# Half of the output projection moved into the second half of attention, keys into its first half, and the next group's weight splits into attention

## The chip, the cores and the metric

The kernel runs on one core of a Trainium2 chip. The metric is the device time of one launch in microseconds (us). Its engines are named as in the profile: PE is TensorE (PEld its weight loads), DVE is VectorE, ACT is ScalarE, POOL is GpSimd and SP is SyncE, which here only issues DMAs.

## The reference

One block of a transformer with adaptive LayerNorm, in fp32, for 4 batches of 512 rows of 1024 features. What matters here is the attention part:

```python
h = _layernorm(x, axis=-1) * (1 + ca) + sa
x = x + ga * _L0_attn_ref(h, L0_attn_wq, L0_attn_wk, L0_attn_wv, L0_attn_wo)
...
q = (x @ wq).reshape(B, S, N_Q_HEADS, HEAD_DIM)
k = (x @ wk).reshape(B, S, N_KV_HEADS, HEAD_DIM)
v = (x @ wv).reshape(B, S, N_KV_HEADS, HEAD_DIM)
q = _rope(q, pos)
k = _rope(k, pos)
...
scores = jnp.where(allowed[None, None, None], scores, neg)
attn = jax.nn.softmax(scores, axis=-1)
out = jnp.einsum('bhgqs,bshd->bqhgd', attn, v).reshape(B, S, N_Q_HEADS * HEAD_DIM)
return out @ wo
```

There are 32 query heads of 128 features, 8 key/value heads (4 query heads to each), and a sliding window of 256 positions. A second LayerNorm and a mixture of 8 low-rank experts with a top-2 gate follow.

## The kernel before

**Precision.** Every large matrix product is made of three: each fp32 operand is split into a high part (rounded to fp32r) and a low part (the rest), and `mm3` (L526) issues high x high, high x low and low x high into one PSUM bank. A weight is split in chunks of 128x1024: the DMA brings it into one of two `stage` buffers, ACT copies it to the high tile (`act_chunk`, L465), POOL subtracts to get the low tile (`pool_chunk`, L476), and this frees the buffer for SP's next load (`sp_chunk`, L408). A group has ten chunks: 0 is V's weights, 1 to 4 are Q's, 5 is the next group's K's, 6 to 9 are those of the output projection.

**Groups.** The work runs in 32 groups, one per batch and key/value head. A group's part of each engine's program is written out by hand, in order, and engines meet only at semaphores. On PE a turn of the loop is: the attention of group n-1 (`pe_attention`), its output projection in eight halves (`pe_wo`; half 2t+c is row tile t, column half c, 12 matmuls of 512 columns), and then the Q, first scores and V of group n (`pe_qv`). A result of a half is in a PSUM bank, and DVE adds it into the SBUF tile `acc` (`dve_wo`, L861) and so frees the bank. Before the change the halves go through banks 2, 3 and 4 in turn (`SBANK`).

**Attention.** It has 16 units: row tile i = u // 4, head u % 4, and 1, 2 or 3 key tiles. A unit's way is: scores on PE; mask and negated maximum on DVE (L878); exponential on ACT (L713); reciprocal and normalise on DVE (L888, `prob <- prob,rrow`); transposes on PE, called the unit's turn (L584); high copy on ACT (L768, `pT_hi`); low part on DVE (L902, `pT_lo`). After four units the values product of the row tile (L595), then ACT's high copy of the output (L779) and DVE's low part (L870), which the output projection reads. PE is three units ahead with scores. The steps of ACT and DVE count s, and at step s:

```python
ACT: pT_hi of unit s-3, exp of unit s, perhaps an output
DVE: mask s, reciprocal s-1, pT_lo of unit s-3, normalise s-1, perhaps an output
```

Between units PE has eight steps of the next group's K projection, three matmuls each, at the units of `K_AT` (0, 1, 2, 3, 5, 7, 12, 13), or of `K_LAST` in a batch's last group, where hT is loaded anew. The values products of row tiles 0 and 1 stand behind units 5 and 9, and those of 2 and 3 behind unit 15.

**Around it.** After attention ACT makes the splits 0 to 5 and the rope of K, then the four ropes of Q with the splits 6 to 9 among them; DVE does the ropes' arithmetic (L845 to L859). In the first four groups of batches 0 to 2 there is also a LayerNorm tile of the next batch: DVE normalises `lx` (`dve_tile`), PE transposes it (`pe_tile`), ACT applies the scale and shift and the high copy (`act_tile`, L740), POOL the low part (`pool_tile`). At the end of a batch `dve_residual` adds the attention's result to x. After the last attention a second phase (`p2_...`) computes the experts.

Of the kernel before, what the change touches and what calls it, by code (L numbers as in the profile page):

```python
# [19 lines left out]
F32 = mybir.dt.float32  # L20
# [23 lines left out]
FAST_N = 256  # L44
LA = 3
# [29 lines left out]
def adaln_block(nc, x, wq, wk, wv, wo, gate_wT, lora_aT, lora_bT, c, wmod, cos, sin, mask, ident, iota, out):  # L75
# [6 lines left out]
    with ExitStack() as top:  # L82
# [329 lines left out]
        def sp_groups(eng, b, rows, store):  # L412

            for t in range(QT):
                n, i = b * KV + 1 + t, b * QT + t
                for j in range(NC):
                    if j == 2:
                        eng.wait_ge(s_pv, QT * n)
                        eng.dma_start(lx[:], rows(t)).then_inc(s_lx, 16)
                    if j == 8 and store:  # L420
                        eng.wait_ge(s_llo, i + 2)
                        for z, tile in enumerate((l_hi, l_lo)):
                            eng.dma_start(hT_d[z][bass.ds((b + 1) * P, P), :, t * P:(t + 1) * P], tile[:].bitcast(F32)).then_inc(s_hst, 16)
                    sp_chunk(eng, n, j)
            with eng.Fori(1 + QT, KV) as g:
# [125 lines left out]

        def pe_wo(eng, n, half):
# [13 lines left out]
        OBANK = [bank[7], bank[1]]  # L566
# [20 lines left out]
        def pe_values(eng, n, i):  # L587
# [64 lines left out]
        def p1_pe(eng):  # L652
            last = BATCH - 1
            with eng.Fori(0, last) as b:
# [3 lines left out]
                for half in range(8):  # L658
# [26 lines left out]
        OUT_STEP = {GQ * i + GQ + 1 + LAG: i for i in range(QT - 2)}  # L685
# [833 lines left out]
```

## Time and profile before

| | |
|---|---|
| median of 3 runs | 2836.81 us (2836.45 to 2838.03) |
| the profiled execution's own time | 2837.69 us |
| its span | 2835.9 us |
| granted TensorE clock, mean | 0.982 |
| busy: PE, DVE, ACT, POOL | 94%, 64%, 49%, 31% |

The span is from the first to the last instruction; the own time lies 1.8 us over it. Busy shares are means over the whole span. A matmul's duration in the rows is longer than the time until the next one starts, because they are pipelined, so the time that PE needs is read from start to start.

### The profile page before, as it was taken

The page shows a single profiled execution, that of the slowest core. Times are in us where ns is not written, and L with a number is a line of the kernel's source. Part 1 is how long each engine was busy: PE and PEld are TensorE (multiplying, and loading weights), DVE is VectorE, ACT ScalarE, POOL GpSimd, SP SyncE. Part 2 cuts the span into 40 slices and gives each one's busy share as a digit, 9 for nine tenths or more (in the row PEclk, how much of TensorE's full clock was granted, in tenths as well). Part 3 has the DMA queues.
Part 4 walks back from the last instruction along what each step waited for, and adds up shares of the span by engine and source line. Part 5 has one row for each costly group of instructions (what it writes and reads, how often), then busy time and mean ns, then how long its engine had stood idle before and what let it go on. Part 6 is the DMA issues. An engine that isn't in the chain of part 4 may idle for free.

```text
span 2835.9 us, 41435 instructions
## 1 busy us (share of the span) xinstructions
PE 2665.6 (94%) x12889; PEld 2159.1 (76%) x12889; DVE 1822.5 (64%) x4131; ACT 1384.9 (49%) x2822; POOL 882.4 (31%) x380
## 2 busy tenths in 40 slices
PE   5799999999899999999899999999899999998999
PEld 3478777777787787777778877877777778776777
DVE  3366666665866666667776666667766676667543
ACT  3255555554455555444455554444454454445341
POOL 2133333322333333332333333333323233333112
PEclk8799999999999999999999999999999999999999
DMA  7622222213333222224223332124222222224211
GB/s 271 223 93 86 89 89 75 67 64 137 111 97 96 90 88 67 69 72 141 98 89 96 96 96 71 63 72 158 90 74 67 73 82 75 74 80 158 90 74 53
DMA packets 169589, 273.21 MB, mean 96 GB/s; under 512 B 8272, under 2 KB 99728, under 8 KB 168208
## 3 DMA queue, kind: packets, MB, share of 16 engines
q1 hardware_dynamic: 164240, 253.05, 27.1%
q10 hardware_dynamic: 5248, 18.91, 1.8%
q8 instruction: 51, 0.84, 0.1%
q14 instruction: 50, 0.41, 0.0%
HBM read 242.54 MB, written 29.39 MB: 96 GB/s over the span
## 4 chain that ended last, share of the span: by engine, by line
PE 54%; DVE 22%; issue 9%; ACT 7%; DMA 1%; ACTq 1%; DVEq 1%; SPq 0%
PE bank L527 17%; PE bank L528 17%; PE bank L529 17%; DVE rotated L849 8%; DVE swapped L846 4%; DVE prob L878 3%; DVE prob L888 3%; ACT swapped L697 2%; PE bank L584 2%; ACT swapped L696 1%; DVE qo_lo L870 1%; ACT w_o_hi L474 1%; ACT prob L713 1%; ACT pT_hi L768 1%; DMA hT_lo<-hT_lo_scratch 1%
## 5 line engine op out<-in xcount | busy, mean ns | idle before, releaser
L479 POOL TENSOR_TENSOR w_o_lo<-stage,w_o_hi 128x1024 fp32r<-128x1024 f32 x128 | 308.7, 2412 | 533.2 <-ACT w_o_hi L474 533.2
L527 PE MATMUL bank<-w_o_hi,qo_hi 128*128 128x512 f32 x1024 | 400.2, 391 | 4.4 <-DVE acc L865 4.4
L527 PE MATMUL bank<-hT_hi,w_q_hi 128*128 128x512 f32 x1024 | 400.5, 391 | 0.5 <-DVE swapped L846 0.2
L528 PE MATMUL bank<-hT_lo,w_q_hi 128*128 128x512 f32 x1024 | 399.2, 390 | 0.0
L529 PE MATMUL bank<-hT_hi,w_q_lo 128*128 128x512 f32 x1024 | 398.9, 390 | 0.0
L529 PE MATMUL bank<-w_o_hi,qo_lo 128*128 128x512 f32 x1024 | 398.5, 389 | 0.0
L528 PE MATMUL bank<-w_o_lo,qo_hi 128*128 128x512 f32 x1024 | 398.5, 389 | 0.0
L479 POOL TENSOR_TENSOR w_q_lo<-stage,w_q_hi 128x1024 fp32r<-128x1024 f32 x128 | 313.6, 2458 | 189.6 <-ACT w_q_hi L474 189.6
L479 POOL TENSOR_TENSOR w_v_lo<-stage,w_v_hi 128x1024 fp32r<-128x1024 f32 x32 | 76.8, 2399 | 933.8 <-ACT w_v_hi L474 933.8
L713 ACT ACTIVATE prob<-prob,nbias 128x384 f32<-128x384 f32 (+2 forms) x512 | 273.7, 535 | 157.5 <-DVE nbias L878 143.6
L865 DVE TENSOR_TENSOR acc<-bank,acc 128x512 f32<-128x512 f32 x256 | 171.7, 687 | 235.7 <-PE bank L529 235.7
L584 PE MATMUL bank<-ident_t,prob 128*128 128x128 f32 x1152 | 222.1, 283 | 90.0 <-DVE prob L888 87.0
L849 DVE TENSOR_TENSOR rotated<-rotated,swapped 128x512 f32<-128x512 f32 x160 | 297.8, 1861 | 5.5
L845 DVE TENSOR_TENSOR rotated<-bank,cos_t 128x512 f32<-128x512 f32 x160 | 110.6, 692 | 285.8 <-ACT swapped L697 285.8
L878 DVE CUSTOM_DVE_ANT_0 prob<-bank,mask_t 128x384 f32<-128x384 f32 (+2 forms) x512 | 229.0, 452 | 69.6 <-PE bank L529 31.5
L584 PEld LDWEIGHTS bank<-ident_t,prob 128*128 128x128 f32 x1152 | 141.0, 141 | 165.6 <-DVE prob L888 131.2
L902 DVE TENSOR_TENSOR pT_lo<-bank,pT_hi 128x384 fp32r<-128x384 f32 (+2 forms) x512 | 228.3, 446 | 37.2 <-ACT pT_hi L768 35.4
L705 ACT ACTIVATE qo_hi<-rotated 128x512 fp32r<-128x512 f32 x128 | 80.8, 631 | 326.7 <-DVE rotated L849 326.7
L768 ACT ACTIVATE pT_hi<-bank 128x384 fp32r<-128x384 f32 (+2 forms) x512 | 204.0, 398 | 54.8 <-PE bank L584 51.1
L527 PEld LDWEIGHTS bank<-hT_hi,w_q_hi 128*128 128x128 f32 x1024 | 192.8, 188 | 44.6 <-issue 2.5
L527 PEld LDWEIGHTS bank<-w_o_hi,qo_hi 128*128 128x128 f32 x1024 | 192.3, 188 | 45.0 <-DVE acc L865 5.7
L529 PEld LDWEIGHTS bank<-hT_hi,w_q_lo 128*128 128x128 f32 x1024 | 192.7, 188 | 40.3
(188 smaller groups left out, 5621.6 us busy)
## 6 DMA issues: line engine op xcount, KB each, us to landing
stage<-in_wq SPq DMA_DIRECT2D x128, 512.0 KB, 3.6
stage<-in_wo SPq DMA_DIRECT2D x128, 512.0 KB, 3.3
stage<-in_wk SPq DMA_DIRECT2D x33, 512.0 KB, 3.6
stage<-in_wv SPq DMA_DIRECT2D x32, 512.0 KB, 3.6
acc<-in_wmod SPq DMA_DIRECT2D x32, 512.0 KB, 5.9
xb<-in_x ACTq DMA_DIRECT2D x20, 512.0 KB, 5.3
wm<-in_wmod SPq DMA_DIRECT2D x8, 1024.0 KB, 12.0
x1s<-x_scratch SPq DMA_DIRECT2D x4, 2048.0 KB, 8.8
```

Of the source, the lines that this page charges most:

```text
L479: eng.tensor_tensor(dst[1], src, dst[0].bitcast(F32), ALU.subtract).then_inc(s_split, 1)
L527: eng.matmul(o, st[0], mv_[0], start=start, stop=False)
L528: eng.matmul(o, st[0], mv_[1], start=False, stop=False)
L529: return eng.matmul(o, st[1], mv_[0], start=False, stop=stop)
L584: m = eng.transpose(bank[5 + u % 2][:, b * P:(b + 1) * P], prob[:, u % GQ, b * P:(b + 1) * P], ident_t[:])
L713: eng.activation(tile, tile, ACT.Exp, bias=nbias[:, u:u + 1], scale=-1.0, accum_out=rowsum[:, u:u + 1]).then_inc(s_exp, 1)
L768: eng.activation(pT[i % 2][0][:, 0:nk, h * P:(h + 1) * P], bank[5 + u % 2][:, 0:nk * P].rearrange("p (b q) -> p b q", q=P), ACT.Copy).then ...
L846: eng.tensor_tensor(swapped[slot][:], swapped[slot][:], sin_t[:], ALU.mult).then_inc(s_rs, 1)
L849: eng.tensor_tensor(rotated[slot][:], rotated[slot][:], swapped[slot][:], ALU.add).then_inc(s_ra, 1)
L865: eng.tensor_tensor(a, SBANK[half % 3][:], a, ALU.add).then_inc(s_wor, 1)
L878: plain(eng.tensor_tensor_reduce(prob[:, u % GQ, 0:w], SBANK[u % 3][:, 0:w], mask_t[:, 3 * P - w:3 * P], -SCALE, FAR, ALU.add, ALU.min, nb ...
L902: eng.tensor_tensor(lo, bank[5 + u % 2][:, 0:nk * P].rearrange("p (b q) -> p b q", q=P), hi.bitcast(F32), ALU.subtract).then_inc(s_ptl, 1)
```

## The change

In attention PE now does the eight K steps at the units 0 to 7 and the first four halves of the group's output projection behind the units 8, 10, 12 and 14. These four halves all use bank1, each after DVE has added the one before; DVE adds them at its steps 12, 14, 16 and 18. All values products use bank7, and that of row tile 2 moves behind unit 13; that of tile 3 stays behind unit 15. The splits 0 to 4 of the next group move into ACT's steps 4, 7, 10, 12 and 14, and split 5 behind ACT's last output. The tile's transposes move from between halves 5 and 6 to behind the first Q projection, ACT's tile behind the first Q rope, POOL's tile behind split 7, SP's load of `lx` behind split 7's load and the tile's store behind the loads. In the last group the second phase's LayerNorm of batch 0 moves into attention's steps.

```diff
+FILL = 4
...
-                    if j == 2:
+                    if j == 8:
                         eng.wait_ge(s_pv, QT * n)
                         eng.dma_start(lx[:], rows(t)).then_inc(s_lx, 16)
...
-                    if ln and j == 5:
+                    if ln and j == 7:
                         pool_tile(eng, b * QT + g - 1)
...
+        def wo_bank(half):
+
+            return bank[1] if half < FILL else SBANK[half % 3]
+
...
-            if half >= 3:
-                eng.wait_ge(s_wor, 8 * n + half - 1)
+            if 1 <= half < FILL:
+                eng.wait_ge(s_wor, 8 * n + half + 1)
+            elif half == FILL + 3:
+                eng.wait_ge(s_wor, 8 * n + FILL + 2)
...
-        OBANK = [bank[7], bank[1]]
+        OBANK = bank[7]
...
-            elif i >= 2:
-                eng.wait_ge(s_ol, QT * n + i - 1)
+            else:
+                eng.wait_ge(s_ol, QT * n + i)
...
-        K_AT = (0, 1, 2, 3, 5, 7, 12, 13)
-
-        K_LAST = (4, 5, 7, 8, 10, 11, 13, 14)
+        K_AT = (0, 1, 2, 3, 4, 5, 6, 7)
+
+        K_LAST = (3, 4, 5, 6, 7, 9, 11, 13)
+        WO_AT = (8, 10, 12, 14)
...
-                if u % GQ == 1 and GQ < u < UNITS - GQ:
+                if u % GQ == 1 and u > GQ:
                     pe_values(eng, n, u // GQ - 1)
-            for i in (QT - 2, QT - 1):
-                pe_values(eng, n, i)
-
-        def pe_qv(eng, n):
+                if u in WO_AT:
+                    pe_wo(eng, n, WO_AT.index(u))
+            pe_values(eng, n, QT - 1)
+
+        def pe_qv(eng, n, tile=None):
             for h in range(GQ):
+                if tile is not None and h == 1:
+                    pe_tile(eng, n - 1, tile)
...
-        OUT_STEP = {GQ * i + GQ + 1 + LAG: i for i in range(QT - 2)}
+        OUT_STEP = {GQ * i + GQ + 1 + LAG: i for i in range(QT - 1)}
+        CHUNK_STEP = {4: 0, 7: 1, 10: 2, 12: 3, 14: 4}
...
-            for j in (0, 1):
-                act_chunk(eng, n, j)
             act_rope(eng, n, 0)
-            for j in (2, 3):
-                act_chunk(eng, n, j)
             if tile is not None:
                 act_tile_sqrt(eng, tile)
-            for j in (4, 5):
-                act_chunk(eng, n, j)
-            if tile is not None:
-                act_tile(eng, tile)
             for r in range(1, 1 + GQ):
                 act_rope(eng, n, r)
+                if r == 1 and tile is not None:
+                    act_tile(eng, tile)
...
-            for i in (QT - 2, QT - 1):
-                act_outputs(eng, n, i)
+                if more and s in CHUNK_STEP:
+                    act_chunk(eng, n + 1, CHUNK_STEP[s])
+                if not more:
+                    act_last(eng, s)
+            act_outputs(eng, n, QT - 1)
+            if more:
+                act_chunk(eng, n + 1, 5)
...
+                if s - 4 in WO_AT:
+                    if s - 4 == WO_AT[0]:
+                        eng.wait_ge(s_acc0, b + 1)
+                    dve_wo(eng, n, WO_AT.index(s - 4))
+            dve_outputs(eng, n, QT - 1)
...
+        def act_last(eng, s):
+
+            if s == 9:
+                act_sqrt2(eng, 0)
+                eng.wait_ge(s_split, 10 * GROUPS + 2)
+            if 12 <= s < 12 + QT:
+                act_normalise2(eng, 0, (s - 12,))
+            if s in (16, 17):
+                eng.wait_ge(u_a, 16)
+                act_a_hi(eng, s - 16)
```

Three places of the order that this makes. On PE, the units 11 and 12 of a group before the change (each: three matmuls of scores, then the turn), with the K step behind unit 12:

```order
L527 MATMUL bank<-kt__hi,qo_hi 128x384
L528 MATMUL bank<-kt__lo,qo_hi 128x384
L529 MATMUL bank<-kt__hi,qo_lo 128x384
L580 REGISTER_ALU
L584 MATMUL bank<-ident_t,prob 128x128 x3
L527 MATMUL bank<-hT_hi,w_k_hi 128x512
L528 MATMUL bank<-hT_lo,w_k_hi 128x512
L529 MATMUL bank<-hT_hi,w_k_lo 128x512
L584 MATMUL bank<-ident_t,prob 128x128 x3
```

The same place after the change, from the scores of unit 15 on; the first matmuls of half 2 stand where the K step stood (12 in all, the same three forms over again):

```order
L528 MATMUL bank<-kt__hi,qo_hi 128x384
L529 MATMUL bank<-kt__lo,qo_hi 128x384
L530 MATMUL bank<-kt__hi,qo_lo 128x384
L587 REGISTER_ALU
L591 MATMUL bank<-ident_t,prob 128x128 x3
L565 REGISTER_ALU
L528 MATMUL bank<-w_o_hi,qo_hi 128x512
L529 MATMUL bank<-w_o_lo,qo_hi 128x512
L530 MATMUL bank<-w_o_hi,qo_lo 128x512
```

On DVE, step 14 after the change (mask of unit 14, reciprocal 13, low part of unit 11, normalise 13); before it is the same without its last row, the add of half 1 into `acc`:

```order
L887 ISA prob,nbias<-bank,mask_t 128x384
L887 ISA nbias 128x1
L892 RECIPROCAL rrow<-rowsum 128x1
L911 TENSOR_TENSOR pT_lo<-bank,pT_hi 128x3x128
L897 TENSOR_SCALAR prob<-prob,rrow 128x384
L872 REGISTER_ALU
L874 TENSOR_TENSOR acc<-bank,acc 128x512
```

On ACT, steps 4 and 5 after the change (high copy of unit 1, exp of unit 4; then the V copy, unit 2, exp of unit 5); the row of `w_v_hi`, split 0, is new between them:

```order
L772 ACTIVATE pT_hi<-bank 128x128
L722 REGISTER_ALU
L723 ACTIVATE prob,rowsum<-prob,nbias 128x256
L469 ISA
L474 ISA
L475 ACTIVATE w_v_hi<-stage 128x1024
L762 ACTIVATE v__hi<-bank 128x512
L772 ACTIVATE pT_hi<-bank 128x128
```

## Rows read from the trace of the kernel before

**Rows 1.** The page: span, and PE's busy time

```profile
span 2835.9 us, 41435 instructions
PE 2665.6 (94%) x12889; PEld 2159.1 (76%) x12889; DVE 1822.5 (64%) x4131; ACT 1384.9 (49%) x2822; POOL 882.4 (31%) x380
```

**Rows 2.** Windows: busy us (instructions) of each engine, PE clock, DMA share, GB/s

```profile
518.90:530.30 11.40, 10.93 (x66) 9.47 (x66) 9.74 (x46) 8.69 (x28) 0.00 (x0) 1.00 0.14 46
530.30:544.90 14.60, 12.70 (x67) 9.82 (x66) 11.38 (x37) 8.46 (x22) 0.00 (x0) 1.00 0.00 0
544.90:597.40 52.50, 52.02 (x237) 42.86 (x236) 29.22 (x40) 21.77 (x34) 23.94 (x10) 1.00 0.30 100
```

**Rows 3.** Waits of 521.4 to 597.4: total us, times, longest

```profile
PEld bank L584 <- DVE prob L888: 3.6, 5, 1.1
```

**Rows 4.** Timeline: start, us, instruction [idle before]; units 8 (529 to 530) and 15

```profile
529.76 0.34 PE L527 MATMUL bank<-kt__hi,qo_hi 128*128 128x384 f32 x1
...
530.29 0.49 PE L584 MATMUL bank<-ident_t,prob 128*128 128x128 f32 x3
...
530.54 0.42 PE L527 MATMUL bank<-kt__hi,qo_hi 128*128 128x384 f32 x1
...
540.39 0.55 PE L584 MATMUL bank<-ident_t,prob 128*128 128x128 f32 x3 [0.71 <-DVE prob L888]
...
540.98 0.49 ACT L768 ACTIVATE pT_hi<-bank 128x384 fp32r<-128x384 f32 x1 [0.76 <-PE bank L584]
...
541.50 0.56 DVE L902 TENSOR_TENSOR pT_lo<-bank,pT_hi 128x384 fp32r<-128x384 f32 x1 [0.70 <-ACT pT_hi L768]
```

**Rows 5.** Timeline: the first of three output-projection matmuls, twice in a row

```profile
405.50 0.39 PE L527 MATMUL bank<-w_o_hi,qo_hi 128*128 128x512 f32 x1
...
406.18 0.39 PE L527 MATMUL bank<-w_o_hi,qo_hi 128*128 128x512 f32 x1
```

**Rows 6.** Groups of 521.4 to 597.4, by form: busy us, mean ns | idle before

```profile
L865 DVE TENSOR_TENSOR acc<-bank,acc 128x512 f32<-128x512 f32 x8 | 5.4, 689 | 10.2 <-PE bank L529 10.2
L888 DVE TENSOR_SCALAR prob<-prob,rrow 128x384 f32<-128x384 f32 x8 | 3.3, 411 | 0.0
L474 ACT ACTIVATE w_q_hi<-stage 128x1024 fp32r<-128x1024 f32 x4 | 4.2, 1054 | 5.1 <-DMA stage<-in_wq 5.1
L479 POOL TENSOR_TENSOR w_q_lo<-stage,w_q_hi 128x1024 fp32r<-128x1024 f32 x4 | 9.5, 2393 | 5.5 <-ACT w_q_hi L474 5.5
```

**Rows 7.** Timeline of a batch change: normalises of units 0 and 1 beside POOL

```profile
755.75 3.52 POOL L512 MEMSET acc<- 128x4096 f32 x1
...
757.35 2.08 DVE L888 TENSOR_SCALAR prob<-prob,rrow 128x128 f32<-128x128 f32 x2
...
759.41 0.47 PE L584 MATMUL bank<-ident_t,prob 128*128 128x128 f32 x1 [3.56 <-DVE prob L888]
```

**Rows 8.** Timeline: end of unit 4's exp, its normalise and its turn

```profile
522.86 0.19 ACT L713 ACTIVATION_READ_ACCUMULATOR prob<-prob,nbias 128x1 f32 x1
...
523.94 0.35 DVE L888 TENSOR_SCALAR prob<-prob,rrow 128x256 f32<-128x256 f32 x1
...
525.22 0.38 PE L584 MATMUL bank<-ident_t,prob 128*128 128x128 f32 x2
```

**Rows 9.** Timeline of ACT, a group with a tile: its affines; ropes 1 and 2

```profile
410.92 2.88 ACT L744 ACTIVATE lf<-bank,modcur 128x128 f32<-128x128 f32 x8
...
420.21 0.59 ACT L696 ACTIVATE swapped<-bank 64x512 f32<-64x512 f32 x1 [5.33 <-PE bank L529]
...
426.23 0.60 ACT L696 ACTIVATE swapped<-bank 64x512 f32<-64x512 f32 x1
```

**Rows 10.** Timeline: first K step after a batch change

```profile
679.13 0.50 PE L527 MATMUL bank<-hT_hi,w_k_hi 128*128 128x512 f32 x1 [1.86 <-DMA hT_lo<-hT_lo_scratch]
```

**Rows 11.** Windows before and after the clock fell, columns as in rows 2

```profile
676.70:680.10 3.40, 1.41 (x6) 1.04 (x7) 2.64 (x12) 1.62 (x6) 0.00 (x0) 1.00 1.01 407
680.10:683.50 3.40, 3.40 (x11) 2.83 (x11) 1.33 (x5) 0.98 (x3) 0.00 (x0) 0.50 1.02 417
```

More of the change, by code:

```diff
@@ L657, in p1_pe @@
                 pe_attention(eng, n, K_LAST, b + 1)
-                for half in range(8):
+                for half in range(FILL, 8):
                     pe_wo(eng, n, half)
@@ L668, in pe_groups @@
                 pe_attention(eng, n - 1, K_AT)
-                for half in range(8):
-                    if ln and half == 6:
-                        pe_tile(eng, n - 1, b * QT + g - 1)
+                for half in range(FILL, 8):
                     pe_wo(eng, n - 1, half)
-                pe_qv(eng, n)
+                pe_qv(eng, n, b * QT + g - 1 if ln else None)
                 if ln:
@@ L984, in p1_dve @@
                 n = b * KV + (KV - 1)
-                dve_wo(eng, n, 0)
                 dve_rope(eng, n + 1, 0)
-                for half in range(1, 8):
+                for half in range(FILL, 8):
                     dve_wo(eng, n, half)
-                    if half in (3, 5):
-                        dve_residual(eng, b, half // 2 - 1, b + 2)
+                    if half in (5, 6):
+                        dve_residual(eng, b, half - 5, b + 2)
                 for t in (2, 3):
@@ L1014, in dve_groups @@
                     dve_tile2(eng, g)
-                    dve_wo(eng, n - 1, 3)
-                for half in range(4, 8):
-                    dve_wo(eng, n - 1, half)
+                    dve_wo(eng, n - 1, 6)
+                dve_wo(eng, n - 1, 7)
                 for r in range(1, 1 + GQ):
@@ L1021, in dve_groups @@
                 n = b * KV + g
-                dve_attention(eng, n - 1)
-                dve_wo(eng, n - 1, 0)
+                dve_attention(eng, n - 1, b)
                 dve_rope(eng, n, 0)
-                for half in range(1, 8):
+                for half in range(FILL, 8):
                     dve_wo(eng, n - 1, half)
@@ L1134, in act_sqrt2, with act_normalise2 @@
             eng.activation(lnv2[:, 1, cols], lnv2[:, 0, cols], ACT.Sqrt).then_inc(u_sq, 1)
-        def act_normalise2(eng, t):
+        def act_normalise2(eng, t, tiles=range(QT)):
             eng.wait_ge(u_x[t % 2], 16 * (t // 2 + 1))
@@ L1141, in act_normalise2 @@
                 eng.wait_ge(u_lnT, KT * t)
[L1142 removed]
+            for i in tiles:
                 g = t * QT + i
[L1144 to L1145 removed]
+                eng.activation(xn[:, i, :], x1s[t % 2][:, i, :], ACT.Identity, bias=lnv2[:, 5, g:g + 1], scale=lnv2[:, 3, g:g + 1]).then_inc(u_xn, 1)
+        def act_last(eng, s):
[7 more added lines that the diff above has]
+                act_a_hi(eng, s - 16)
         def act_ln2_chunk(eng, t, k):
@@ L1226, in dve_stats2, with dve_chain2 @@
             plain(eng.bn_aggr(dst, st2[:, t, :, :].rearrange("p a s -> p (a s)"))).then_inc(s_st2, 1)
-        def dve_chain2(eng, r, between):
+        def dve_chain2(eng, r, part):
             cols = slice(QT * r, QT * (r + 1))
@@ L1233, in dve_chain2 @@
             base = CHAIN * r
-            eng.wait_ge(s_st2, STATS2 + 3 * QT * r)
-            eng.tensor_scalar(lv[0], m[:, :, 1], EPS, None, ALU.add).then_inc(u_ln, 1)
-            between()
+            if part == 0:
+                eng.wait_ge(s_st2, STATS2 + 3 * QT * r)
+                eng.tensor_scalar(lv[0], m[:, :, 1], EPS, None, ALU.add).then_inc(u_ln, 1)
+                return
             eng.wait_ge(u_sq, r + 1)
@@ L1321, in p2_dve @@
             res = lambda t: dve_residual(eng, BATCH - 1, t, BATCH + 1)
-            dve_chain2(eng, 0, lambda: dve_wo(eng, LAST, 0))
-            for half in range(1, 4):
-                dve_wo(eng, LAST, half)
-            res(0)
             for half in range(4, 8):
@@ L1343, in p2_dve @@
                         dve_stats2(eng, i, x1s[t1 % 2][:, i, :], mv2[:, t1, i, :], STATS2 + 3 * QT * t + 3 * i)
-                    dve_chain2(eng, t1, lambda: None)
-                dve_us(eng, t, 1)
+                        if i == 1:
+                            dve_us(eng, t, 1)
+                    for part in range(2):
+                        dve_chain2(eng, t1, part)
+                else:
+                    dve_us(eng, t, 1)
                 dve_us(eng, t, 2)
@@ L1423, in p2_pe @@
         def p2_pe(eng):
-            for half in range(8):
-                if half >= 4:
-                    pe_ln2_chunk(eng, 0, half - 4)
+            for half in range(FILL, 8):
                 pe_wo(eng, LAST, half)
+                pe_ln2_chunk(eng, 0, half - FILL)
             for t in range(BATCH):
```

69 lines of the change are left out of this document (33 added, 36 removed).

## The prediction

> **What bounds the kernel now.** I read the page first. TensorE (PE) is busy 94% of a span of 2835.9 us [rows 1], so no more can be won than its pauses, and the question is where they lie. In a plain group (one without LayerNorm work; 521.4 to 597.4 us, from V's transposes to those of the next group, 76.0 us) the windows say: from the end of V to the first output-projection matmul PE is busy 10.93 of 11.40 us and then 12.70 of 14.60 us; in the remaining 52.5 us it pauses for 0.5 us [rows 2]. The waits name the cause: PE's weight load waits for the normalise of VectorE (DVE), 3.6 us in five waits [rows 3]. One of the five stands before unit 0 and is not touched by the change. The others, counted from start to start of matmuls between units 9 and 15, is 2.8 us. All that the change can take from attention is thus 2.8 us x 31 = 87 us. Everything else depends on which waits the moved work brings along.
>
> **The new second half of attention.** Durations first. Three 512-column matmuls start 0.68 us apart, so a half of 12 costs 2.72 us [rows 5]. A unit's scores take 0.53 us and its three transposes 0.25 us [rows 4]. After a turn (transposes) starts, ACT's copy begins 0.59 us later and DVE's low part 0.52 us after that [rows 4]; that subtraction holds DVE about 0.46 us, the normalise behind it 0.33 us (its 411 ns less the overlap with its successor), and the add into acc 0.69 us [rows 6].
>
> Each half in attention writes bank1, and its PE wait asks that DVE has added the half before. DVE does that add at the end of its step u+4, behind the low part of unit u+1. So PE must turn unit 9 before half 1, unit 11 before half 2, unit 13 before half 3, and then stand until 0.59 + 0.52 + 0.46 + 0.33 + 0.69 + 0.05 = 2.64 us have gone by since that turn. What PE has to do meanwhile:
> - half 1: turn 9, two key tiles of values (1.45), scores 13, turn 10: 2.55 us. Wait 0.1.
> - half 2: turn 11 (0.25), scores 15 (0.6), turn 12 (0.25): 1.1 us. Wait 1.5.
> - half 3: turn 13, three key tiles of values (2.04), turn 14: 2.7 us. Wait 0.
> - values 3 now stand directly behind turn 15, where before values 2 covered it. They need the low part of unit 15: 0.59 + 0.52 + 0.56 + 0.1 = 1.75 us after the turn, of which the turn covers 0.3. Wait 1.45.
>
> That is 3.05 us, against the 2.8 us that vanish. The second half gains nothing even before ACT and GpSimd (POOL) take on the weight splits.
>
> **The splits in attention.** Per group five copies on ACT (1.05 us) and five subtractions on POOL (2.39 us) come into attention, at ACT steps 4, 7, 10, 12 and 14; the sixth follows attention as before [rows 6]. While POOL runs, the adds and the masks, whose one large input is in PSUM, keep their time (the eight adds average 689 ns in a group whose splits run beside them [rows 6]). The normalise reads and writes SBUF. Where POOL's memset of acc ran over it, two of 128 columns took 2.08 us in place of some 0.5, and PE's next turn waited 3.56 us [rows 7]; the same happened at each of the three batch changes. In the middle of attention no normalise meets POOL in the trace of before. The bounds for one meeting are therefore 0 and the rest of a 2.39 us subtraction, and I take the full rest, because the row nearest in operation shows it.
>
> On this place the Trainium skill ("SBUF — State Buffer", Who interferes with whom) says two things: a VectorE instruction in a two-port mode and a GpSimd one shut each other out for the whole instruction, while one with at most one SBUF input outside those modes does not contend. By the first, the sum below stands; by the second, the splits would cost only ACT's copies, and the sum would be that of rival A. The row on the memset agrees with the first.
>
> Step by step, with dense PE times from the trace [rows 4, 8]:
> - Split 0 (ACT step 4). ACT is free at 523.05, copies to 524.1, and POOL runs to 526.55. The copy of unit 2's transposes starts at 524.7 (the V copy of 0.6 us stands ahead of it); its low part ends 525.27; the normalise of unit 4, at 523.94 before, is held until 526.75. PE wants it at 525.22 and turns at 526.85: 1.6 us. DVE then owes the V low part, a mask and a low part, and unit 5 is 0.35 us late.
> - Split 1 (step 7) holds the normalise of unit 7: 1.25 us. Half 0 then waits 0.2 us for output 0.
> - Split 2 (step 10) holds that of unit 10 until DVE is 1.0 us late for half 1: 1.1 us, the 0.1 included. Split 3 (step 12) holds unit 12 and half 2 waits 1.85 us, the 1.5 included. Split 4 (step 14) holds unit 14 while PE is in values 2 and half 2: 0.1 us at half 3. Values 3: 1.45 us.
>
> New waits: 1.6 + 0.35 + 1.25 + 0.2 + 1.1 + 1.85 + 0.1 + 1.45 = 7.9 us. Less 2.8 us: 5.1 us more per attention, x 31 = **158 us**. The two K steps that move from units 12 and 13 into units 4 and 6 cost the same PE time there; counted in these starts.
>
> **The LayerNorm tile.** In the first four groups of batches 0 to 2 (12 in all) ACT's tile (eight affines of 2.88 us in all, a high copy of 1.06 us, together 4.0 us [rows 6, 9]) moves from the wo section to behind the first Q rope. The four ropes already run 6.02 us apart [rows 9] against 24 x 0.227 = 5.44 us of PE per projection, and their end releases unit 0. So the 4.0 us are not hidden: they push every later rope, and POOL's low part of the tile, now behind split 7, meets DVE's next SBUF subtraction (about 0.7 us, estimate). PE's own eight tile transposes (0.9 us) now fall into the same stretch and cover that much. 4.0 + 0.7 - 0.9 = 3.8 us, x 12 = **46 us**, seen as waits ahead of Q3, V and unit 0.
>
> **Batch changes and tail.** At a batch change K's first step, now at unit 3 and not 4, still waits for the same DMA, which ended a wait of 1.86 us at 679.13 [rows 10]; neutral. The gate row ga is requested after attention as before, but only four halves (10.9 us of PE) now lie ahead of Q0, not eight, so the residual ends later against Q0: some 3 to 4 us (estimate), 3 x 3.6 = **11 us**. In the last attention, which has no K steps, four halves fill real pauses, with the same bank1 waits and four normalise copies on ACT in between; with the earlier start of the second phase I take **-4 us**, bounds -15 and +5.
>
> Sum: 158 + 46 + 11 - 4 = +211 us. The profiled execution itself took 2837.69 us and the runs' median is 2836.81, so the sum reads 3048; I write 3045.
>
> **The rivals.**
> - A, the splits don't hold DVE: normalises pass POOL freely. Then only ACT's copies delay (0.5 us at unit 4, 0.2 later) and the waits are 3.05 + 0.2 + 0.7 = 3.95, 1.15 us over the old 2.8: 31 x 1.15 = 36, + 46 + 7 = 2925 us. For it: the adds under POOL. Against it: the memset row.
> - B, faster: the halves fill the pauses and DVE, with a whole half's slack, runs ahead. PE then loses 2.8 us per attention: 2837 - 87 = 2750 us if the tile is also hidden. It decides if the new waits stay under 1.0 us per attention (2.8 less 57 / 31 for the other terms). For it: in the second half DVE has only some 12.5 us of work in 22 us of PE. Against it: the wait on bank1 is a round trip, not a load, and at half 2 PE has 1.1 us to cover 2.64.
> - C, the clock: where the waits stand close, PE falls to 1.2 GHz. After 676.7 to 680.1, PE busy 1.41 of 3.40 us, the granted clock was 0.50 for the next 3.4 us [rows 11]; the pause at unit 4 with its follower looks much like that stretch. 3.4 us at half clock cost up to 1.7 us: in every attention +53, 3100 us.
> - D, nothing to tell from no change (0.2%, about what a measurement of this kernel resolves): gains and losses cancel.
>
> **How the numbers follow.** Forecast (slower by 5 to 9%) 0.64, its own range 2975 to 3090; A 0.15; B 0.09; C 0.09; D 0.03. Range 2895 to 3105: it takes in A and half of C. Faster 0.09, same 0.03, slower 0.88.
>
> **What would show it.** PE waits on DVE's normalise (unit 4 and 7) of over 1 us, that normalise lasting 1.2 to 2.2 us beside a POOL subtraction; a PE wait of 1.5 to 2 us for DVE's acc at half 2; one of 1.3 to 1.6 us for pT_lo ahead of values 3; plain group 81 us, tile group 85 to 86 us (it now has 0.9 us more than the plain one, the transposes of the tile). It is wrong if the normalise keeps 0.41 us under POOL (then A), or if DVE adds half 1 before PE has turned unit 12 (then B).

## The result and the profile after

The changed kernel takes 3003.8 us (median of 4 runs, 3001.3 to 3004.3) against 2836.6 us: slower by 5.9%, ratio 1.0587, 95% interval 1.0569 to 1.0605. The prediction's 3045 us was 41 us too high.

The page of the kernel after, its span, busy times and, of the groups that it lists, those with the waits of PE. It answers to [rows 1]. Line numbers have moved: L591 is the turn, L528 the first product of every three, L897 the normalise, L874 the add into acc, L911 pT_lo, L480 POOL's part of a split.

```profile
span 2999.5 us, 41441 instructions
PE 2700.0 (90%) x12889; PEld 2179.4 (73%) x12889; DVE 1969.9 (66%) x4131; ACT 1365.5 (46%) x2822; POOL 877.4 (29%) x380
...
L528 PE MATMUL bank<-w_o_hi,qo_hi 128*128 128x512 f32 x1024 | 412.4, 403 | 58.5 <-DVE acc L874 58.3
...
L528 PE MATMUL bank<-hT_hi,w_q_hi 128*128 128x512 f32 x1024 | 405.0, 396 | 19.8 <-DVE swapped L855 19.8
L897 DVE TENSOR_SCALAR prob<-prob,rrow 128x384 f32<-128x384 f32 (+2 forms) x512 | 408.0, 812 | 0.0
...
L591 PE MATMUL bank<-ident_t,prob 128*128 128x128 f32 x1152 | 216.2, 278 | 78.8 <-DVE prob L897 78.8
```

PE has as many instructions as before and 34 us more of busy time, but its share fell from 94 to 90%. DVE has as many instructions too and is busy for 147 us more: its work has not grown, but some of its instructions are held up while they run. The first and the last of the PE groups in the kernel before:

```profile
L527 PE MATMUL bank<-w_o_hi,qo_hi 128*128 128x512 f32 x1024 | 400.2, 391 | 4.4 <-DVE acc L865 4.4
...
L584 PE MATMUL bank<-ident_t,prob 128*128 128x128 f32 x1152 | 222.1, 283 | 90.0 <-DVE prob L888 87.0
```

PE's pauses for the normalise did not grow in sum: 87.0 us before, 78.8 after. The old ones (2.8 us per attention) went, and new ones at other units came. What grew is PE's wait for the add into acc (4.4 to 58.3 us) and for the ropes (0.2 to 19.8 us ahead of Q, 3.4 to 27.4 ahead of V), and 37.5 us for pT_lo ahead of the values products are new.

Windows of one plain group, which answer to [rows 2]: units 1 to 10, units 11 to 15, and the rest up to the next V transposes. Each row gives the length, then the busy us (instructions) of PE, PEld, DVE, ACT and POOL, and then PE's clock.

```profile
633.80:653.50 19.70, 17.22 (x94) 14.27 (x92) 17.00 (x53) 13.00 (x36) 7.15 (x3) 1.00 0.21 64
653.50:669.70 16.20, 13.65 (x67) 11.01 (x67) 11.67 (x26) 6.91 (x15) 4.80 (x2) 1.00 0.26 84
669.70:713.60 43.90, 42.82 (x195) 35.29 (x196) 25.68 (x37) 16.69 (x29) 12.04 (x5) 1.00 0.21 64
```

Attention now holds four halves (10.9 us of PE) and still has 5.0 us of pauses in 35.9 us; the two attention windows of [rows 2] held 2.4 us of pauses in 26.0. The clock stays at 1.00, so in the plain groups rival C's mechanism is absent.

The timeline of that attention shows each wait. Columns as in [rows 4].

```profile
636.46 2.37 POOL L480 TENSOR_TENSOR w_v_lo<-stage,w_v_hi 128x1024 fp32r<-128x1024 f32 x1 [6.38 <-ACT w_v_hi L475]
...
637.27 1.72 DVE L897 TENSOR_SCALAR prob<-prob,rrow 128x256 f32<-128x256 f32 x1
...
639.04 0.44 PE L591 MATMUL bank<-ident_t,prob 128*128 128x128 f32 x2 [1.29 <-DVE prob L897]
...
643.02 1.97 DVE L897 TENSOR_SCALAR prob<-prob,rrow 128x256 f32<-128x256 f32 x1
...
645.05 0.44 PE L591 MATMUL bank<-ident_t,prob 128*128 128x128 f32 x2 [0.74 <-DVE prob L897]
...
653.64 0.50 PE L528 MATMUL bank<-w_o_hi,qo_hi 128*128 128x512 f32 x1 [0.59 <-DVE acc L874]
...
657.03 0.49 PE L591 MATMUL bank<-ident_t,prob 128*128 128x128 f32 x3
...
658.88 0.68 DVE L874 TENSOR_TENSOR acc<-bank,acc 128x512 f32<-128x512 f32 x1
...
659.62 0.50 PE L528 MATMUL bank<-w_o_hi,qo_hi 128*128 128x512 f32 x1 [1.24 <-DVE acc L874]
...
668.02 0.49 PE L591 MATMUL bank<-ident_t,prob 128*128 128x128 f32 x3
...
669.07 0.56 DVE L911 TENSOR_TENSOR pT_lo<-bank,pT_hi 128x384 fp32r<-128x384 f32 x1 [1.77 <-ACT pT_hi L772]
669.68 0.50 PE L528 MATMUL bank<-pT_hi,v__hi 128*128 128x512 f32 x1 [1.17 <-DVE pT_lo L911]
```

At unit 4 POOL runs from 636.46 to 638.83. The normalise, 0.35 us for this width in [rows 8], starts at 637.27 and ends at 638.99, just behind it, and PE turns at 639.04. Unit 7 is the same. Then come half 1, half 2 (from turn 11 at 657.03 to the half at 659.62: 2.59 us, of which PE has work for 1.1) and values 3. Counted from start to start of matmuls, less the matmul's own time, the five waits are 1.45, 0.91, 0.81, 1.46 and 1.39 us.

In a group with a LayerNorm tile two more stand behind the ropes, 0.87 us ahead of Q3 (Q0 to Q3 are the four query projections) and 2.42 ahead of V:

```profile
371.45 0.50 PE L528 MATMUL bank<-hT_hi,w_q_hi 128*128 128x512 f32 x1 [0.70 <-DVE swapped L855]
...
380.20 0.55 PE L528 MATMUL bank<-hT_hi,w_v_hi 128*128 128x512 f32 x1 [2.26 <-DVE swapped L855]
```

All groups, from V's transposes to the next ones, us:

| stretch | before | after | difference |
|---|---|---|---|
| 16 plain groups | 76.13 each | 79.71 each | 57.3 |
| 12 tile groups | 77.08 each | 84.69 each | 91.3 |
| 3 batch changes | 89.5 each | 93.7 each | 12.6 |
| prologue to the first attention | 137.5 | 135.5 | -2.0 |
| last attention and second phase | 287.0 | 291.3 | 4.3 |

The sum is 163.5 us, and the spans differ by 163.6.

### The profile page after: what moved, and what is told of

Read it like the earlier page. It is cut to its first block, busy times and chain, and to the rows that moved or that the text cites. A ratio compares the mean times of both kernels' runs of the same rounds, so it can differ in the third digit from the quotient of the medians.

```text
span 2999.5 us, 41441 instructions
## 1 busy us (share of the span) xinstructions
PE 2700.0 (90%) x12889; PEld 2179.4 (73%) x12889; DVE 1969.9 (66%) x4131; ACT 1365.5 (46%) x2822; POOL 877.4 (29%) x380
## 4 chain that ended last, share of the span: by engine, by line
PE 55%; DVE 22%; issue 9%; ACT 8%; DMA 2%; ACTq 1%; DVEq 0%; SPq 0%
PE bank L528 18%; PE bank L529 17%; PE bank L530 17%; DVE rotated L858 7%; DVE prob L897 5%; DVE swapped L855 4%; PE bank L591 3%; ACT swapped L707 2%; DVE acc L874 1%; ACT lf L748 1%; ACT swapped L706 1%; DVE prob L887 1%; DMA ga_t<-mod_scratch 1%; ACT pT_hi L772 1%; DVE pT_lo L911 1%
## 5 line engine op out<-in xcount | busy, mean ns | idle before, releaser
L480 POOL TENSOR_TENSOR w_o_lo<-stage,w_o_hi 128x1024 fp32r<-128x1024 f32 x128 | 308.6, 2411 | 823.9 <-ACT w_o_hi L475 823.9
L528 PE MATMUL bank<-w_o_hi,qo_hi 128*128 128x512 f32 x1024 | 412.4, 403 | 58.5 <-DVE acc L874 58.3
L480 POOL TENSOR_TENSOR w_q_lo<-stage,w_q_hi 128x1024 fp32r<-128x1024 f32 x128 | 306.7, 2396 | 455.4 <-ACT w_q_hi L475 455.4
L528 PE MATMUL bank<-hT_hi,w_q_hi 128*128 128x512 f32 x1024 | 405.0, 396 | 19.8 <-DVE swapped L855 19.8
L897 DVE TENSOR_SCALAR prob<-prob,rrow 128x384 f32<-128x384 f32 (+2 forms) x512 | 408.0, 812 | 0.0
L911 DVE TENSOR_TENSOR pT_lo<-bank,pT_hi 128x384 fp32r<-128x384 f32 (+2 forms) x512 | 229.8, 449 | 220.9 <-ACT pT_hi L772 218.6
L591 PE MATMUL bank<-ident_t,prob 128*128 128x128 f32 x1152 | 216.2, 278 | 78.8 <-DVE prob L897 78.8
L858 DVE TENSOR_TENSOR rotated<-rotated,swapped 128x512 f32<-128x512 f32 x160 | 272.8, 1705 | 5.5
L528 PEld LDWEIGHTS bank<-w_o_hi,qo_hi 128*128 128x128 f32 x1024 | 192.1, 188 | 113.6 <-DVE acc L874 72.5
L528 PEld LDWEIGHTS bank<-hT_hi,w_q_hi 128*128 128x128 f32 x1024 | 193.7, 189 | 68.6 <-DVE swapped L855 26.6
L591 PEld LDWEIGHTS bank<-ident_t,prob 128*128 128x128 f32 x1152 | 147.5, 141 | 128.6 <-DVE prob L897 105.3
L529 PEld LDWEIGHTS bank<-hT_lo,w_q_hi 128*128 128x128 f32 x1024 | 193.9, 189 | 39.6
```

Source lines behind the costliest of these rows:

```text
L480: eng.tensor_tensor(dst[1], src, dst[0].bitcast(F32), ALU.subtract).then_inc(s_split, 1)
L528: eng.matmul(o, st[0], mv_[0], start=start, stop=False)
L529: eng.matmul(o, st[0], mv_[1], start=False, stop=False)
L591: m = eng.transpose(bank[5 + u % 2][:, b * P:(b + 1) * P], prob[:, u % GQ, b * P:(b + 1) * P], ident_t[:])
L858: eng.tensor_tensor(rotated[slot][:], rotated[slot][:], swapped[slot][:], ALU.add).then_inc(s_ra, 1)
L897: plain(eng.tensor_scalar(tile, tile, rrow[:, u:u + 1], None, ALU.mult)).then_inc(s_nrm[u % GQ], 1)
```

## The experiments

"Plain" below is the mean of the 16 plain groups. Each ratio is to the kernel before, run on the same chip.

**1. What the splits cost: work cut to a corner.** In `act_chunk` (calls from attention) and `pool_chunk` for the chunks 0 to 5:

```diff
+            if narrow:
+                dst, src = sl(dst, lambda d: d[:, 0:1, 0:32]), src[:, 0:1, 0:32]
```

> The changed kernel, but from group 1 on the splits of w_v, w_q and w_k take only a corner of 32 columns of one k, on ScalarE and on GpSimd; the rest of these weights' high and low parts is left as the first group made it (their loads and every wait stay). My theory: the splits cost the attention its waits ahead of unit 4 (1.45 us), unit 7 (0.91) and most of half 1 (0.7 of 0.81), while half 2 (about 1.5) and values 3 (1.4) stay, since these come of one bank and of nothing behind unit 15. A plain group then takes 79.7 - 3.0 = 76.7 us and the kernel some 3004 - 31 x 3.0 = 2911 us (2895 to 2935). Rival (the splits' cost is small, the halves' order costs nearly all): the waits at units 4 and 7 stay, 2985 or more.

Measured: 2908.5 us, ratio 1.0253 (1.0233 to 1.0272), plain 76.35. The waits left in a plain group are 1.47 us ahead of half 2 and 1.39 ahead of values 3; those at units 4 and 7 and at half 1 are gone. The expectation (2911) held, and the rival fell. Without the splits, the halves in attention leave a plain group at 76.35 against 76.13 us: they gain nothing, as the prediction had it.

The same with only POOL's part cut:

> As the kernel with both parts narrow, but ScalarE copies its whole chunk again (1.05 us) and only GpSimd's subtraction is cut to the corner; most of the low parts of w_v, w_q and w_k is left as the first group made it. My theory: nearly all of the splits' price is VectorE's normalise standing beside GpSimd, so the time is within 15 us of the kernel with both narrow, some 2911 to 2926 us, with normalises of 0.35 to 0.41 us. Rival (ScalarE's copy ahead of an exp is what makes PE wait): 2960 to 3004, near the changed kernel.

Measured: 2920.7 us, ratio 1.0289 (1.0269 to 1.0309), plain 76.58; inside the range, and the rival fell. So of the 3.36 us that the splits add to a plain group (79.71 less 76.35), ScalarE's copies are 0.23 and POOL's subtractions 3.13. The groups by form of the normalise, first in the kernel after (a plain group), then here:

```profile
L897 DVE TENSOR_SCALAR prob<-prob,rrow 128x384 f32<-128x384 f32 x8 | 7.5, 933 | 0.0
...
L897 DVE TENSOR_SCALAR prob<-prob,rrow 128x256 f32<-128x256 f32 x4 | 4.4, 1096 | 0.0
```

```profile
L899 DVE TENSOR_SCALAR prob<-prob,rrow 128x384 f32<-128x384 f32 x8 | 3.3, 410 | 0.0
L899 DVE TENSOR_SCALAR prob<-prob,rrow 128x256 f32<-128x256 f32 x4 | 1.4, 348 | 0.0
```

**2. One half of the change at a time.** First the splits alone, on the kernel before (`CHUNK_STEP`, the calls behind it, and the order on SP that they need):

```diff
+                if more and s in CHUNK_STEP:
+                    act_chunk(eng, n + 1, CHUNK_STEP[s])
```

> The kernel before with one part of the change: the splits of the next group in the attention, at the same steps; the output projection, the banks, K and the values stay as before (the load of lx and the stores of the LayerNorm tile stand later on SP, as in the change, since they would block the loads otherwise). My theory: new waits of about 1.45 us ahead of unit 4 and 0.9 ahead of unit 7, and 0 to 2 us ahead of units 10 to 15, so a plain group of 78.4 to 80.4 us and 2837 + 31 x (2.4 to 4.4) = 2911 to 2973 us, I take 2930. Rival (splits are hidden): 2837 within 10.

Measured: 3192.0 us, ratio 1.1246 (1.1226 to 1.1267), plain 88.15. My theory had the direction and missed the size by a factor of four. The timeline and three windows behind one of the splits:

```profile
598.39 2.34 POOL L479 TENSOR_TENSOR w_q_lo<-stage,w_q_hi 128x1024 fp32r<-128x1024 f32 x1 [2.94 <-ACT w_q_hi L474]
...
599.20 1.75 DVE L888 TENSOR_SCALAR prob<-prob,rrow 128x384 f32<-128x384 f32 x1
...
601.00 0.90 PE L584 MATMUL bank<-ident_t,prob 128*128 128x128 f32 x3 [2.88 <-DVE prob L888]
```

```profile
597.70:601.00 3.30, 0.42 (x3) 0.10 (x1) 2.27 (x3) 1.97 (x5) 2.34 (x1) 0.98 0.21 82
601.00:607.60 6.60, 4.61 (x17) 3.29 (x18) 5.59 (x15) 3.50 (x8) 2.36 (x1) 0.75 0.31 90
607.60:611.10 3.50, 3.50 (x11) 2.77 (x10) 1.05 (x2) 0.49 (x1) 0.00 (x0) 0.52 0.33 130
```

With no halves between the units nothing covers a held normalise. Each of the five splits makes PE wait here (1.44, 1.58, 1.34, 3.05 and 1.78 us ahead of turns, and four smaller waits of 0.4 to 0.7 us behind them). Behind some of them the granted clock falls to the lower level (1.2 GHz), where 512-column matmuls start 0.43 us apart and not 0.23. The middle row of the windows is a mixture: the clock was 0.51 from 601.0 to 604.4, then 1.00 up to 607.6 with PE busy for 1.21 of 3.20 us, and then 0.52. That is rival C's mechanism, in a kernel with longer pauses.

Then the halves alone, on the kernel after (the load of lx on SP is put back too):

```diff
+            for j in (0, 1):
+                act_chunk(eng, n, j)
             act_rope(eng, n, 0)
+            for j in (2, 3):
+                act_chunk(eng, n, j)
...
+            for j in (4, 5):
+                act_chunk(eng, n, j)
```

> The changed kernel with its splits of w_v, w_q and w_k back behind the attention, in the order in which the kernel before had them. My theory: no wait ahead of units 4 and 7, 1.5 us ahead of half 2, 1.4 ahead of values 3; but only 4 halves (10.9 us) stand ahead of Q0, and the fourth w_q split ended some 19 us behind the attention before, so Q0 waits about 3.9 us for it. A plain group takes 79.7 - 3.0 + 3.9 = 80.6 us, and the kernel some 3030 us (2990 to 3070). Rival (splits cost nothing in the attention): 3004 + 31 x 3.9 = 3125 us.

Measured: 3059.1 us, ratio 1.0772 (1.0749 to 1.0796), plain 81.65; inside the range, 29 us over the value. The normalises are at 411 ns again, half 2 waits 1.47 and values 3 1.39, and behind attention PE waits for an add ahead of a half and, inside Q0, for the last split of Q's weights, which the four halves no longer cover:

```profile
599.82 0.50 PE L528 MATMUL bank<-w_o_hi,qo_hi 128*128 128x512 f32 x1 [1.57 <-DVE acc L876]
...
609.35 0.50 PE L528 MATMUL bank<-hT_hi,w_q_hi 128*128 128x512 f32 x1 [2.44 <-POOL w_q_lo L480]
```

The second wait is the expected one, but 2.6 us (start to start) and not 3.9. The first, 1.7 us, was not in the expectation. Nor was the clock: in 14 of the 16 plain groups six to eight 512-column matmuls stand 0.43 us apart, and these groups take 81.4 to 82.2 us; the two without any take 79.7 and 80.4.

So, over 2837: splits alone +355 us, halves alone +222, both +167. The parts pay for each other: the halves need the splits out of the way of Q0, and the splits need the halves as cover.

**3. Each wait by itself.** The splits later in attention:

```diff
-        CHUNK_STEP = {4: 0, 7: 1, 10: 2, 12: 3, 14: 4}
+        CHUNK_STEP = {10: 0, 12: 1, 14: 2, 16: 3, 18: 4}
...
             act_rope(eng, n, 0)
+            act_chunk(eng, n, 5)
```

> The changed kernel with the five splits of the attention later, at steps 10, 12, 14, 16 and 18 instead of 4, 7, 10, 12 and 14, and w_k's behind the first rope; the load of lx before the sixth chunk. My theory (only a normalise that stands beside GpSimd in a part with no half to hide it costs): the waits ahead of units 4 and 7 go (1.45 and 0.91), 3004 - 31 x 2.36 = 2931 us (2920 to 2960). Rival (each split costs its wait wherever it stands, as in the kernel with the splits alone, where five cost 11.9 us a group): 3000 or more.

Measured: 2916.4 us, ratio 1.0288 (1.0271 to 1.0305), plain 76.60. This is 15 us below the value and 4 us below the range: the waits at units 4 and 7 went as expected, and the 0.81 us ahead of half 1 too. The rival fell. The 256-column normalises are free of POOL now, but the 384-column ones meet it as often as in the changed kernel (mean 937 ns, 933 there). Here is one of them. PE waits for none that the trace shows; half 2 has its wait for the bank (1.6 us), under which the split at step 12 is hidden:

```profile
555.82 2.41 POOL L480 TENSOR_TENSOR w_q_lo<-stage,w_q_hi 128x1024 fp32r<-128x1024 f32 x1 [3.20 <-ACT w_q_hi L475]
556.63 1.81 DVE L896 TENSOR_SCALAR prob<-prob,rrow 128x384 f32<-128x384 f32 x1
```

The add into acc at the head of VectorE's step:

```diff
             for s in range(EARLY + 1, UNITS + LAG):
+                if s - 4 in WO_AT:
+                    if s - 4 == WO_AT[0]:
+                        eng.wait_ge(s_acc0, b + 1)
+                    dve_wo(eng, n, WO_AT.index(s - 4))
                 if s < UNITS:
                     dve_mask(eng, n, s)
...
-                if s - 4 in WO_AT:
-                    if s - 4 == WO_AT[0]:
-                        eng.wait_ge(s_acc0, b + 1)
-                    dve_wo(eng, n, WO_AT.index(s - 4))
```

> The changed kernel with one line moved: VectorE adds a half of the attention onto acc at the head of its step (ahead of the mask of the same step) instead of at its end behind pT_lo, normalise and qo_lo. My theory (one bank, whose release stands behind a unit's whole chain, makes half 2 wait): the 1.46 us ahead of half 2 and most of the 0.81 ahead of half 1 go, units 4 and 7 and values 3 keep theirs; plain group 79.7 - 2.2 = 77.5 us, kernel 3004 - 31 x 2.2 = 2936 us (2930 to 2970). Rival (one bank alone is the limit, wherever the add stands, since the mask behind it comes later): 2990 to 3020.

Measured: 2973.0 us, ratio 1.0486 (1.0468 to 1.0503), plain 78.93. That is 31 us of the expected 68, 3 us outside the range and below the rival's. Half 1's wait went. Ahead of turn 12 PE now waits 0.64 us and ahead of half 2 still 0.9 of its 1.46 us: this is split 3, which the bank's round trip (the add's way from the turn to the free bank) had hidden:

```profile
571.02 2.39 POOL L480 TENSOR_TENSOR w_q_lo<-stage,w_q_hi 128x1024 fp32r<-128x1024 f32 x1 [3.55 <-ACT w_q_hi L475]
571.83 1.80 DVE L897 TENSOR_SCALAR prob<-prob,rrow 128x384 f32<-128x384 f32 x1
...
573.56 0.68 DVE L879 TENSOR_TENSOR qo_lo<-bank,qo_hi 128x512 fp32r<-128x512 f32 x1
...
574.16 0.67 DVE L874 TENSOR_TENSOR acc<-bank,acc 128x512 f32<-128x512 f32 x1
574.88 0.50 PE L528 MATMUL bank<-w_o_hi,qo_hi 128*128 128x512 f32 x1 [0.65 <-DVE acc L874]
```

Half 4 as cover for unit 15's pT_lo:

```diff
...
+            if cover:
+                pe_wo(eng, n, FILL)
             pe_values(eng, n, QT - 1)
```

> The changed kernel, but half 4 stands between unit 15's turn and values 3 instead of behind values 3. My theory (values 3 waits for pT_lo of unit 15 since nothing stands between them): the 1.39 us ahead of values 3 go and nothing else moves, 3004 - 31 x 1.39 = 2961 us (2950 to 2975). Rival (half 4 waits for qo_lo of values 2, or half 6 for qo_lo of values 3, in its place): 2985 to 3004.

Measured: 3044.1 us, ratio 1.0737 (1.0719 to 1.0755), 40 us slower than the change. The wait ahead of values 3 went, but half 7 shares its bank with half 4, whose add stands behind the K rope on DVE:

```profile
607.43 1.88 DVE L876 TENSOR_TENSOR acc<-bank,acc 128x512 f32<-128x512 f32 x3
...
608.17 0.68 PE L528 MATMUL bank<-w_o_hi,qo_hi 128*128 128x512 f32 x1 [1.94 <-DVE acc L876]
```

The rival was right in kind (the wait moves on), but not in place or size. Nine of the 16 plain groups take 82.0 to 82.2 us and the others 80.2 to 80.6. In each of the nine, seven or eight 512-column matmuls stand 0.43 us apart, in the others none; in one of the nine the granted clock was 0.52 for 3.4 us behind that pause.

The tile's place:

```diff
-                if tile is not None and h == 1:
+                if tile is not None and h == 0:
                     pe_tile(eng, n - 1, tile)
...
                 act_tile_sqrt(eng, tile)
+                act_tile(eng, tile)
```

> The changed kernel with only the LayerNorm tile's place moved back, as far as it can be: its transposes ahead of Q0 instead of behind it, ScalarE's eight activations and copy ahead of Q0's rope instead of behind it, VectorE's tile ahead of half 5's and 6's adds. My theory (the 4.05 us that a tile group takes beyond a plain one are the 0.87 ahead of Q3 and the 2.42 ahead of V, both the 4 us of ScalarE's tile handed on from rope to rope): 12 x 3.3 = 40 us go, 3004 - 40 = 2964 us (2955 to 2985), and the plain groups stay at 79.7. Rival (the tile itself costs this wherever it stands, or VectorE's tile is not ready and Q0 waits for it): 2990 or more.

Measured: 3009.5 us, ratio 1.0595 (1.0577 to 1.0613), tile groups 85.3 us against 84.7; the rival held. The waits at Q3 and V went, and PE waited ahead of the tile's transposes in their place, since DVE's tile (behind the K rope) ends at 440.4:

```profile
439.60 0.81 DVE L982 TENSOR_SCALAR lx<-lx,lnv 128x1024 f32<-128x1024 f32 x1
...
440.55 1.96 PE L550 MATMUL bank<-ident_t,lx 128*128 128x128 f32 x8 [3.51 <-DVE lx L982]
```

**4. All together.** The four moves in one kernel:

> The early add, half 4 ahead of values 3 and the late splits together, and the LayerNorm tile's transposes ahead of Q0, its ScalarE part ahead of Q0's rope, and VectorE's part of the tile ahead of half 5's add. My theory: the five waits add up and go, 79.7 - 6.0 = 73.7 us for a plain group, and of the tile groups' own 4.05 us some 3 go: 3004 - 31 x 6.0 - 12 x 3 = 2782 us (2770 to 2815), faster than the kernel before (2837). Rival (with the waits gone VectorE itself becomes the bound of the attention, or the waits move on): 2837 or more.

Measured: 2849.6 us, ratio 1.0043 (1.0029 to 1.0058), plain 75.06, tile groups 78.8. The expectation missed by 68 us, and the rival's second form (the waits move on) held. It is better than the kernel before in the plain groups, not as a whole: half 2 kept 0.76 us (split at step 12) and half 7 waited 0.68, or 2.41 in a tile group. Both repaired (splits at steps 10, 14, 16, 18 and behind attention; half 4's add ahead of qo_lo of values 3):

> All four moves, with two repairs from the run of them: half 4's add ahead of qo_lo of values 3 (half 7 had waited 0.68 us for it in a plain group, 2.75 in a tile group, since it stood behind a rope and the tile's statistics), and no split at step 12 (its GpSimd part held normalise 12, qo_lo and the add, and half 2 had waited 0.76); splits at steps 10, 14, 16, 18 and behind the attention. My theory: a plain group of 74.95 - 0.68 - 0.76 = 73.5 us, a tile group of 79.2 - 2.75 - 0.76 = 75.7 us, and 2849.6 - 19 x 1.44 - 12 x 3.5 = 2780 us (2770 to 2805), 2% below the kernel before. Rival (the waits move on to the next step, as they did twice): 2810 or more.

Measured: 2839.4 us, ratio 0.9999 (0.9989 to 1.0010); the rival held again. The plain group came out as worked out (73.34), the tile groups did not (79.7): PE, now earlier, waited 3.4 us for DVE's tile. So the last step starts that tile ahead of the K rope (against the kernel just above; the rest is told in the expectation):

```diff
...
                     def between():
-                        dve_wo(eng, n - 1, 5)
+                        dve_rope(eng, n, 0, True, 0)
                         eng.wait_ge(s_lsq, i + 1)
                     dve_tile(eng, i, between)
+                    dve_rope(eng, n, 0, True, 1)
+                    dve_wo(eng, n - 1, 5)
```

> The kernel of all moves, with VectorE's part of the LayerNorm tile started ahead of the K rope (statistics, then the rope up to its sum while ScalarE takes the root, then the tile, then the rope's low part), lx loaded earlier on SP, and at a batch change the four residuals spread between the adds and the ropes. My theory: PE waited 3.4 us ahead of the tile's transposes in each of 12 groups, and up to 7.6 us ahead of Q3 at a batch change, for VectorE's order alone; the tile is then ready at about 417 us on the run's own clock, when PE comes to it. Tile groups of 79.5 go to about 75.3 us, batch changes from 94.6 to about 90.5, so 2839.4 - 12 x 4.2 - 3 x 4 = 2777 us (2765 to 2800), 2% below the kernel before. Rival (the tile's work on VectorE and ScalarE has no room left in so short a group, and the wait moves on to Q3 and V): 2810 or more.

Measured: 2775.6 us (5 runs, 2770.2 to 2778.5), ratio 0.9770 (0.9757 to 0.9784): 2.3% faster than the kernel before. Plain 73.41, tile groups 74.57, batch changes 94.1. These had stood at 94.6 and gained almost nothing of the expected 4 us: the wait that the expectation puts ahead of Q3 stands ahead of Q2, and 5.4 to 5.8 us of it are left. Its page, and PE at the tile, which it reaches without a wait:

```profile
span 2776.7 us, 41448 instructions
PE 2650.1 (95%) x12889; PEld 2174.7 (78%) x12889; DVE 1849.9 (67%) x4131; ACT 1383.5 (50%) x2822; POOL 878.1 (32%) x380
...
L528 PE MATMUL bank<-w_o_hi,qo_hi 128*128 128x512 f32 x1024 | 413.9, 404 | 0.8 <-DVE acc L880 0.7
...
402.05 0.81 DVE L991 TENSOR_SCALAR lx<-lx,lnv 128x1024 f32<-128x1024 f32 x1
...
403.33 1.03 PE L550 MATMUL bank<-ident_t,lx 128*128 128x128 f32 x8
```

## Why the prediction was right, and where its sizes were off

- **Direction and mechanism held.** Of 512 normalises 155 ran beside a subtraction of POOL, and all 155 ended 0.15 to 0.22 us behind its end; experiment 1 shows that the subtractions cost 3.13 us of a plain group. Rival A (2925) falls with it. The Trainium skill ("SBUF — State Buffer", Who interferes with whom) has a two-port VectorE instruction and a GpSimd one shut each other out for the whole instruction. The trace agrees in the direction that it shows: in all 155 POOL had begun first, and the normalise was held until it had ended. That the normalise runs in such a mode, no run shows by itself. Of the signs that the prediction named, the length of the normalise (1.72 and 1.97 us), the waits at unit 4 and values 3 came as said; unit 7 (over 1 us, measured 0.91), half 2 (1.5 to 2, 1.46), the plain group (81, 79.7) and the tile group (85 to 86, 84.7) fell just short.
- **The attention term, 158 us, was mis-sized: 31 x 3.58 = 111 us.** It is off by 47 us, more than the whole forecast is (211 us predicted; 111 + 48 + 2 + 4 - 2 = 163 by these bullets). The prediction's new waits of 7.9 us were 6.0. Unit 4 (1.6, measured 1.45), values 3 (1.45, 1.39), half 1 (1.1, 0.81), half 2 (1.85, 1.46) and unit 7 (1.25, 0.91) were all too high, and the carry-overs to unit 5, half 0 and half 3 (0.35, 0.2, 0.1) did not come: I added each split's delay to the next wait, and by the trace the steps between took it up. At half 2 the split's 0.35 us and the bank's 1.5 are not added: with the splits cut to a corner, half 2 still waits 1.47. The loss of the 2.8 us of old waits was right. The waits account for 6.0 - 2.8 = 3.2 of the 3.58 us; the other 0.4 us stand in no wait of over 0.15 us, and I have no cause for them.
- **"The second half gains nothing even before the splits"** was right: 76.35 against 76.13 us.
- **The tile term, 46 us: 91.3 - 12 x 3.58 = 48 us.** Waits came ahead of Q3 and V, as said, but no new one ahead of unit 0; together they are 3.3 us, and not 3.8. That the sum fits is in part luck, since the clock, which this term left out, fell behind the wait ahead of V in seven of the 12: they take 84.9 to 85.0 us, the others 84.0 to 84.6. Windows of the kernel after, that wait and what follows:

```profile
293.00:295.40 2.40, 0.11 (x1) 0.11 (x1) 2.37 (x2) 0.00 (x0) 1.69 (x1) 0.95 1.01 286
295.40:298.80 3.40, 3.40 (x9) 2.68 (x10) 1.68 (x6) 2.76 (x4) 1.15 (x1) 0.53 0.94 258
```

- **Batch changes: +11 predicted**, 12.6 - 3 x 3.58 = 2 us beyond the share of a plain attention. The wait behind the residuals came nearly as priced, but ahead of Q2 and not of Q0: PE is idle there for 4.4, 3.4 and 3.3 us in the three, and not at all before. In the first, DVE waits for ga and then has the residuals ahead of Q0's rope, which frees the bank that Q2 writes:

```profile
768.20 1.23 DVE L1045 TENSOR_TENSOR acc<-acc,ga_t 128x1024 f32<-128x1024 f32 x1 [3.49 <-DMA ga_t<-mod_scratch]
...
782.50 0.50 PE L528 MATMUL bank<-hT_hi,w_q_hi 128*128 128x512 f32 x1 [4.42 <-DVE swapped L855]
```

  K's DMA was not neutral: PE is idle 3.3 to 3.6 us for it, 1.9 to 2.5 before. Against this, 1.1 to 1.2 us ahead of V and about 1.1 us ahead of a half went, and the attention at a batch change, with its K steps elsewhere, shows no wait at units 4 and 7 or at half 1, so it costs less than 3.58 us. None of this was tried by itself.
- **Tail: -4 predicted, +4.3.** The last attention has waits of 1.5 and 1.6 us ahead of halves 1 and 2 and of 1.4 ahead of values 3. Of the second phase, counted from the last V transposes, the gate's products start only 1.0 us earlier than before, and the first products of the experts (`aT`) 3.2 us later. So the gain from filled pauses and the earlier start did not come; why the experts start later was not tried. The prologue is 2 us shorter, for which I have no cause.
- **Rival B (faster) named the right condition**, "DVE, with a whole half's slack, runs ahead": in the late-splits kernel the stalls are still there, and its plain group (76.60 us) is that of the kernel without POOL's subtractions (76.58). It failed in the change because two splits stand in the units that have no half, and because the releases that half 1, half 2 and values 3 wait for stand late in the order. At half 2 and values 3 this is so without the splits too; half 1's wait takes both, and went with either. With these orders and the places of the splits and the tile changed, the last kernel takes 2775.6 us against 2840.0 for the kernel before on the same chip.

## What to carry to other kernels

Work put under a busy engine's time costs by the slack of the engine that it slows at that place, not by its length: the same 2.4 us subtraction cost a wait of 0.9 to 3.1 us where units followed each other, and nothing behind most blocks of 2.7 us. At step 12 it cost nothing only while half 2 had a longer wait of its own, and 0.8 us once that was gone. When several waits are in series, removing one may only show the next, so move them together and read the trace again: two of the four moves lost time or gained none by themselves, and the repaired set is worth 228 us against the change. For each buffer that is reused once per block, write down what stands on the releasing engine's queue ahead of the release.

## What was not expected of the hardware

Not every VectorE instruction is held beside POOL's subtraction. The add into acc (PSUM and SBUF) kept 0.69 us in 216 meetings with POOL in the kernel before, and pT_lo of three key tiles (PSUM and SBUF) its 0.56 us in 93 in the kernel after; the normalise of that width went from 0.41 to 1.81 us in 93. The rope's sum of two SBUF operands took 2.77 us all 78 times that it met POOL, against 0.69 us alone. In the kernel before it met POOL 90 times, under the query projections. POOL's own subtraction kept 2.4 us in nearly all of them. The clock was 0.51 after PE had been busy 0.42 us of 3.30, 0.52 after 1.21 of 3.20 (both in the kernel with the splits alone) and 0.53 after 0.11 of 2.40 (kernel after), while pauses of 0.8 to 1.5 us, five to an attention, left it at 1.00.
